# Key sums of an attention kernel: from products with ones on the matrix engine to block transpositions on the vector engine

## What is computed

```
q, k, v = xn @ Wq + bq, xn @ Wk + bk, xn @ Wv + bv     # xn = layernorm(x)
attn = softmax(q @ k.T / 8)                             # over 2048 keys
x = x + layernorm((attn @ v) @ Wo + bo)
```

## Time and profile before

| | us |
|---|---|
| median of 3 runs | 2374.09 (2373.32 to 2374.96) |
| profiled execution | 2373.21 |
| its span | 2371.2 |
| TensorE busy (matmul) | 2339.9 |
| GpSimd busy | 2118.6 |
| VectorE busy | 2064.4 |
| ScalarE busy | 1378.1 |

### The profile page before, as it was taken

The page is one execution under the profiler, slowest core; times in us unless marked ns, Lnnn a source line. Parts: engine busy times, 40 slices in busy tenths (PEclk is TensorE's granted clock), DMA queues, the critical chain, the costliest instruction groups (busy, mean ns, idle before and its releaser), DMA issues.

```text
span 2371.2 us, 43568 instructions
## 1 busy us (share of the span) xinstructions
PE 2339.9 (99%) x15676; PEld 1183.6 (50%) x15676; DVE 2064.4 (87%) x3164; ACT 1378.1 (58%) x1666; POOL 2118.6 (89%) x1220
## 2 busy tenths in 40 slices
PE   8999999999999999999999999999999999999997
PEld 4454554554554545545545545554554544544454
DVE  7888888888888888888888888888888888889987
ACT  6656555555555655655565655656556565555546
POOL 7998989989898989989989898988989988899986
PEclk9999999999999999999999999999999999999999
DMA  2000000000000000100010000100000000110101
GB/s 60 28 17 26 28 24 23 28 21 22 28 29 18 28 24 18 33 28 15 28 31 17 28 28 15 32 28 15 28 28 19 28 28 15 35 33 19 37 28 36
DMA packets 63895, 62.54 MB, mean 26 GB/s; under 512 B 29796, under 2 KB 47588, under 8 KB 63684
## 3 DMA queue, kind: packets, MB, share of 16 engines
q1 hardware_dynamic: 62820, 59.51, 8.3%
q10 hardware_dynamic: 864, 0.26, 0.0%
HBM read 56.88 MB, written 2.61 MB: 25 GB/s over the span
## 4 chain that ended last, share of the span: by engine, by line
PE 92%; POOL 5%; DVE 2%; issue 1%; ACT 0%; DMA 0%; POOLq 0%; DVEq 0%; ACTq 0%
PE o_ps L466 36%; PE spare_ps L421 14%; PE score_ps L445 10%; PE score_ps L451 9%; PE score_ps L448 9%; POOL total L1211 4%; PE spare_ps L407 3%; PE spare_ps L389 3%; PE spare_ps L398 3%; PE spare_ps L511 3%; PE spare_ps L478 1%; DVE max_part L929 1%; DVE ln_stats L901 0%; POOL y_acc L1261 0%; PE score_ps L559 0%
## 5 line engine op out<-in xcount | busy, mean ns | idle before, releaser
L1211 POOL TENSOR_TENSOR total<-total,probs 128x832 f32<-128x832 f32 (+1 forms) x896 | 1761.7, 1966 | 218.4 <-ACT probs L738 142.9
L929 DVE TENSOR_REDUCE max_part<-spare_ps 128x1 f32<-128x512 f32 x2028 | 1303.9, 685 | 261.8 <-PE spare_ps L421 247.9
L738 ACT ACTIVATE probs<-score_ps 128x1024 f32<-128x1024 f32 x1024 | 993.2, 1022 | 812.6 <-PE score_ps L451 812.6
L466 PE MATMUL o_ps<-probs,v_sb 128*64 128x512 f32 x4096 | 979.7, 599 | 0.0
L466 PEld LDWEIGHTS o_ps<-probs,v_sb 128*64 128x64 f32 x4096 | 265.9, 136 | 451.3 <-issue 287.0
L421 PE MATMUL spare_ps<-k_hi,q_hi 64*128 64x512 f32 x2028 | 461.4, 449 | 7.6 <-DVE max_part L929 4.4
L445 PE MATMUL score_ps<-q_hi,kd_hi 64*128 64x512 f32 x2048 | 407.0, 393 | 0.9 <-ACT score_ps L728 0.9
L421 PEld LDWEIGHTS spare_ps<-k_hi,q_hi 64*128 64x128 f32 x2028 | 193.2, 183 | 428.1 <-issue 226.9
L451 PE MATMUL score_ps<-q_hi,kd_lo 64*128 64x512 f32 x2048 | 405.3, 391 | 0.0
L448 PE MATMUL score_ps<-q_lo,kd_hi 64*128 64x512 f32 x2048 | 404.1, 390 | 0.0
L972 DVE TENSOR_REDUCE part_sum<-probs 128x192 f32<-128x768 f32 (+1 forms) x255 | 392.5, 1539 | 1.3 <-ACT probs L738 1.2
(11 more groups left out here) (145 smaller groups left out, 1174.0 us busy)
## 6 DMA issues: line engine op xcount, KB each, us to landing
m_all<-m_scratch SPq DMA_DIRECT2D x64, 512.0 KB, 4.3
denom<-denom_scratch SPq DMA_DIRECT2D x122, 128.0 KB, 2.9
m_scratch<-neg_rows SPq DMA_DIRECT2D x256, 1.0 KB
y_acc<-in_L_attn_x SPq DMA_DIRECT2D x8, 256.0 KB, 6.3
key_f<-in_L_attn_x SPq DMA_DIRECT2D x8, 256.0 KB, 2.7
block_out<-probs SPq DMA_DIRECT2D x8, 256.0 KB, 2.3
denom_col<-denom SPq DMA_DIRECT2D x61, 4.0 KB
denom_scratch<-denom_col SPq DMA_DIRECT2D x61, 4.0 KB, 1.4
```

What stands on the lines that cost most here:

```text
L466: last = nc.tensor.matmul(o_ps[half(h), :], v_sb[:, b, kt, half(h)], probs[:, st % RING, h, :], start=(kt == 0), stop=(kt == T - 1))
L738: nc.scalar.activation(probs[:, st % RING], score_ps[st % 2][:], ACT.Exp, scale=SCALE).then_inc(s["exp_done"], 1)
L929: nc.vector.reduce_max(max_part[:, G % 2, h, qt, kc:kc + 1], bank[max_bank(n, h)], AX.X).then_inc(s["max_done"], 1)
L1211: nc.gpsimd.tensor_tensor(others(total[:, G % 2], G), so_far, others(probs[:, st % RING], G), ALU.add).then_inc(s["sum_done"], 1)
```

## The change

For chunks 0 to 55 (`TURNED` = 64 - 8) the sum over partitions is made without TensorE. VectorE's block transposition turns each 32x32 block of `total` (128x1024) in place of its own (`dve_turn`, into `q_parts`, which is free at that time); a sum along groups of 32 elements gives, for each quarter of the partitions, the sums of 1024 columns (`dve_row_sums`, 128x32); a second transposition (128x32) lays them in rows; four DMAs put the four quarters beside each other on 128 partitions (`sp_quarters`), where VectorE adds them and takes the reciprocal (`dve_quarters`). From there the way is the old one. Chunks 56 to 60 keep the products with ones, and the last three their own way.

Besides, places change: keys d = 4 to 3 (in the first unit 6 and 4 to 3), values 5 to 4, merge 2 to 1, the last part sum of a chunk 1 to 0. For the turned chunks the transposition stands at d = 2, row sums at 4, quarters, reciprocal and the broadcast of the reciprocals at 7, the scaling at d = 4 of the chunk after the next and the output projection at its d = 6. Queries stay at 2. The waits of the old way count from chunk 56 on.

```
-MERGE_AT, L_AT, DENOM_OUT_AT, RECIP_AT, NEG_MAX_AT, NORM_AT = 2, 3, 4, 5, 4, 7
+K_AT = {(0, 3): 0, (1, 0): 1, (1, 3): 2, (2, 3): 3}
+V_AT = {(0, 4): (0, 4), (1, 4): (4, 4), (2, 4): (8, 4), (3, 4): (12, 4)}
+MERGE_AT, L_AT, DENOM_OUT_AT, RECIP_AT, NEG_MAX_AT, NORM_AT = 1, 3, 4, 5, 4, 7
-PART_AT = {3: 0, 5: 1, 6: 2, 1: -1}
+PART_AT = {3: 0, 5: 1, 6: 2, 0: -1}
+TURNED = CHUNKS - 2 * NC
+TURN_AT, ROW_SUM_AT, QUARTERS_OUT_AT, QUARTERS_AT, TURNED_NORM_AT, TURNED_WO_AT = 2, 4, 4, 7, 4, 6
...
+def by_products(G):
+    return TURNED <= G < CHUNKS - COLUMN_CHUNKS
+def by_blocks(G):
+    return 0 <= G < TURNED
...
+        def dve_turn(dve, G):
+            dve.wait_ge(s["sum_done"], (G + 1) * ADDS)
+            dve.wait_ge(s["merge_done"], G + 1)
+            if G:
+                dve.wait_ge(s["rows_summed"], G)
+            else:
+                dve.wait_ge(s["first_split"], FIRST_Q)
+            nc.vector.transpose(q_parts[:].rearrange("p c n -> p (c n)"),
+                                total[:, G % 2].rearrange("p h n -> p (h n)")).then_inc(s["sums_turned"], 1)
+        def dve_row_sums(dve, G):
+            dve.wait_ge(s["sums_turned"], G + 1)
+            if G:
+                dve.wait_ge(s["rows_turned"], G)
+            nc.vector.tensor_reduce(row_sum[:], q_parts[:].rearrange("p c (b i) -> p (c b) i", i=32), AX.X, ALU.add).then_inc(s["rows_summed"], 1)
+            dve.wait_ge(s["rows_summed"], G + 1)
+            if G:
+                dve.wait_ge(s["quarters_in"], 64 * G)
+            nc.vector.transpose(row_turned[:], row_sum[:]).then_inc(s["rows_turned"], 1)
+        def dve_quarters(dve, G):
+            dve.wait_ge(s["quarters_in"], 64 * (G + 1))
+            if G:
+                dve.wait_ge(s["scratch_dma"], 16 * G)
+            nc.vector.tensor_reduce(denom_col[:], denom_quarters[:].rearrange("p a k -> p k a"), AX.X, ALU.add).then_inc(s["quarters_added"], 1)
+            dve.wait_ge(s["quarters_added"], G + 1)
+            nc.vector.reciprocal(denom_col[:], denom_col[:]).then_inc(s["recip_done"], 1)
...
+        def sp_quarters(sp, G):
+            sp.wait_ge(s["rows_turned"], G + 1)
+            if G:
+                sp.wait_ge(s["quarters_added"], G)
+            for a in range(P // 32):
+                sp.dma_start(denom_quarters[:, a, :], row_turned[a * 32:(a + 1) * 32, :]).then_inc(s["quarters_in"], 16)
```

More of the change, by code:

```diff
@@ L63 @@
 WEIGHTS_AT = 2
-FIRST_K_AT = {(0, 6): 0, (1, 0): 1, (1, 4): 2, (2, 4): 3}
-FIRST_V_AT = {(0, 5): (0, 4), (1, 5): (4, 4), (2, 5): (8, 4), (3, 5): (12, 4)}
+FIRST_K_AT = {(0, 3): 0, (1, 0): 1, (1, 3): 2, (2, 3): 3}
+FIRST_V_AT = {(0, 4): (0, 4), (1, 4): (4, 4), (2, 4): (8, 4), (3, 4): (12, 4)}
 FIRST_Q = Q_RING
@@ L108, in projected_at @@
 def projected_at(G, d):
-    if d == WO_AT and 2 <= G < CHUNKS + 2 - COLUMN_CHUNKS:
+    if G < 2:
+        return None
+    if d == (TURNED_WO_AT if G - 2 < TURNED else WO_AT) and G - 2 < CHUNKS - COLUMN_CHUNKS:
         return G - 2
     return None
+def by_products(G):
+    return TURNED <= G < CHUNKS - COLUMN_CHUNKS
+def by_blocks(G):
+    return 0 <= G < TURNED
 def ffn_at(n, stage):
@@ L151, in spare_banks @@
             use("p", g)
-        if d == L_AT and 0 < G <= CHUNKS - COLUMN_CHUNKS:
+        if d == L_AT and by_products(G - 1):
             use("L", G - 1)
@@ L207, in build @@
         denom_4 = sb("denom_4", [P, CH // 2])
+        row_sum = sb("row_sum", [P, 32])
+        row_turned = sb("row_turned", [P, 32])
+        denom_quarters = sb("denom_quarters", [P, P // 32, 2 * TC])
         denom_col = sb("denom_col", [P, CH // HD])
@@ L359, in take @@
                 elif was == "L":
-                    pe.wait_ge(s["denom_copied"], k + 1)
+                    pe.wait_ge(s["denom_copied"], k + 1 - TURNED)
                 elif was == "Wo":
@@ L746, in act_denom @@
         def act_denom(act, G):
-            act.wait_ge(s["denom_ps_ready"], G + 1)
-            if G:
-                act.wait_ge(s["col_dma"], 16 * G)
+            act.wait_ge(s["denom_ps_ready"], G + 1 - TURNED)
+            if G > TURNED:
+                act.wait_ge(s["col_dma"], 16 * (G - TURNED))
             nc.scalar.activation(denom_4[:], bank[SPARE["L", G]][:, 0:CH // 2], ACT.Copy).then_inc(s["denom_copied"], 1)
@@ L974, in dve_part, with total_taken @@
                                     AX.X, ALU.add).then_inc(s["part_done"], 1)
+        def total_taken(eng, G):
+            if by_blocks(G):
+                eng.wait_ge(s["sums_turned"], G + 1)
+            else:
+                eng.wait_ge(s["denom_ps_ready"], G + 1 - TURNED)
+        def dve_turn(dve, G):
[3 more added lines that the diff above has]
+                dve.wait_ge(s["rows_summed"], G)
+            else:
+                dve.wait_ge(s["first_split"], FIRST_Q)
[17 more added lines that the diff above has]
+            nc.vector.reciprocal(denom_col[:], denom_col[:]).then_inc(s["recip_done"], 1)
         def dve_merge(dve, G):
@@ L997, in dve_recip @@
         def dve_recip(dve, G):
-            dve.wait_ge(s["col_dma"], 16 * (G + 1))
+            dve.wait_ge(s["col_dma"], 16 * (G + 1 - TURNED))
             nc.vector.reciprocal(denom_col[:], denom_col[:]).then_inc(s["recip_done"], 1)
@@ L1095, in dve_columns @@
         def dve_columns(dve, G):
-            dve.wait_ge(s["denom_ps_ready"], G + 1)
+            dve.wait_ge(s["denom_ps_ready"], G + 1 - TURNED)
             nc.vector.reciprocal(recip_col[:, G % 2, :], bank[SPARE["L", G]][:, 0:2 * TC]).then_inc(s["denom_copied"], 1)
         def dve_head_y(dve, G):
-            dve.wait_ge(s["denom_copied"], G + 1)
+            dve.wait_ge(s["denom_copied"], G + 1 - TURNED)
             dve.wait_ge(s["wo_ps_ready"], G + 1)
@@ L1134, in dve_program @@
                     dve_centre(dve)
-                if d == RECIP_AT and 0 < G <= CHUNKS - COLUMN_CHUNKS:
+                if d == QUARTERS_AT and by_blocks(G - 1):
+                    dve_quarters(dve, G - 1)
+                if d == RECIP_AT and by_products(G - 1):
                     dve_recip(dve, G - 1)
@@ L1156, in dve_program @@
                     dve_q(dve, G + 2)
+                if d == TURN_AT and by_blocks(G - 1):
+                    dve_turn(dve, G - 1)
+                if d == ROW_SUM_AT and by_blocks(G - 1):
+                    dve_row_sums(dve, G - 1)
                 if n in HEADS_AT:
@@ L1205, in pool_add @@
                 if G >= 2:
-                    pool.wait_ge(s["denom_ps_ready"], G - 1)
+                    total_taken(pool, G - 2)
                 so_far = others(probs[:, (st - 1) % RING], G)
@@ L1336, in pool_program @@
                 G, u, c, d = n // PER_CHUNK, n // (PER_CHUNK * NC), n // PER_CHUNK % NC, n % PER_CHUNK
-                if d == NORM_AT and 0 < G <= CHUNKS - COLUMN_CHUNKS:
+                if d == TURNED_NORM_AT and by_blocks(G - 2):
+                    norm(pool, G - 2)
+                if d == NORM_AT and by_products(G - 1):
                     norm(pool, G - 1)
@@ L1404, in sp_denom_back @@
             sp.wait_ge(s["recip_done"], G + 1)
+            sp.wait_ge(s["denom_dma"], 32 * G)
             sp.dma_start(denom_dram.rearrange("h (p n) -> (h p) n", p=HD), denom_col[:]).then_inc(s["scratch_dma"], 16)
@@ L1452, in sp_program @@
                     sp_ffn_weights(sp)
-                if d == DENOM_OUT_AT and 0 < G <= CHUNKS - COLUMN_CHUNKS:
+                if d == DENOM_OUT_AT and by_products(G - 1):
                     sp_denom_out(sp, G - 1)
@@ L1456, in sp_program @@
                     sp_m_out(sp, G + 1)
-                if d == RECIP_AT and 0 < G <= CHUNKS - COLUMN_CHUNKS:
+                if d == RECIP_AT and by_products(G - 1):
                     sp_denom_back(sp, G - 1)
+                if d == QUARTERS_OUT_AT and by_blocks(G - 1):
+                    sp_quarters(sp, G - 1)
                 if d == M_BACK_AT and G + 1 < CHUNKS:
                     sp_m_back(sp, G + 1)
+                if d == QUARTERS_AT and by_blocks(G - 1):
+                    sp_denom_back(sp, G - 1)
                 for g in ffn_at(n, ST1):
```

9 lines of the change are left out of this document (4 added, 5 removed).

## The result

The changed kernel takes 2393.8 us in the median (five runs, 2391.95 to 2396.98) against 2375.0 for the one before on the same chip: ratio 1.0075, 95% interval 1.0064 to 1.0086. It is slower by 19 us, where 11 us less were forecast.

The account below looks back on a forecast made before the run. TensorE, with 92% of the span, was taken as the bound. Savings of 0.57 and 0.12 us less new stalls gave -0.18 us a chunk, times 56 is -10 us: 2373.2 to 2363 us, range 2350 to 2384.

Parts of the forecast that it names:

- rival 1: Double step 4: row sums run at the part sums' rate, 2.03 us instead of 1.22; 2393 us; chance 0.18, transposition included.
- lateness: Time in us from TensorE's start of a double step's first trial-product pair to VectorE's start on it.
- steps 1, 2 and 6: Double steps of a chunk's attention loop, each opened by a late VectorE; predicted losses 0.09, 0.12 and 0.12 us.
- step 3: Double step after low query and large transposition, which were to make VectorE 0.92 us late; predicted cost 0.12 us.
- the floor: The 0.54 us from TensorE's start of the first pair to VectorE's when VectorE is on time; costs nothing.
- step 7: Double step after output sum and part sum beside the output projection; VectorE at most 0.68 us late, old 0.12 loss gone.
- plain: Said of a double step with no projection; a part sum there was to cost the next double step 0.12 us.
- Rival 2: Stalls in two places, for instance double steps 2 and 4, eat all the gain: 2373 us; 0.14 including a disturbed transfer.
- Rival 3: VectorE's one large item per double step does not stall TensorE: 2335 us; chance 0.12 with what lies toward it.

Follow-up runs that it names:

- the first experiment: The changed kernel with its new places but no block transpositions, all key sums by products with ones on TensorE: 2423.4 us, ratio 1.0194 against the kernel before.

## Why the prediction was wrong

*What held.* TensorE in the loop is the bound. The durations: transposition 1.24 forecast, 1.234 measured; row sums 1.22 and 1.178, so rival 1 did not come. The lateness that each step leaves: 0.89 in steps 1, 2 and 6 (measured 0.88 to 0.90), 0.92 in step 3 (0.95), the floor in 5. (At step 7 it is the floor too, where at most 0.68 was forecast: step 6 lasted longer, so VectorE caught up.) The 0.57 of the products stands in the first experiment's chain. That its chunk of 36.22 is 0.56 longer than the changed one's 35.66 is in part chance, for it loses 0.23 at step 3, and the changed kernel 0.25 at steps 3 and 4. Transfers and GpSimd's additions delayed nothing in the loop.

*The step that failed* is the first one: "So the loss is zero up to about 0.7, 0.12 at 0.89, and above that lateness less 0.80". The 0.12 came from the earlier trace rows, from a step 7 in which no projection stands. I carried it to steps 2, 3 and 6, where one does. There it is 0.17 for queries, 0.20 for keys, 0.17 for values, and 0.29 for outputs, because the projection has a wait of its own, for the bank of A1; the extra 0.1 of the outputs stays open. Steps 2, 3 and 6 have 0.65 together instead of 0.36: 0.29 a chunk. Rows that could have told me stood in my own trace, but I read there a pair without a projection. At step 5 of chunks 58 and 59, beside a value projection, latenesses of 0.99 and 1.22 cost 0.26 and 0.53, where my rule gives 0.19 and 0.42.

*The second step that failed*: "Before, the part sum was plain here, and its 0.12 is gone." It went from step 7 and came back at step 0 as a wait for the seed, 0.10 a chunk. Together 0.39, which is the difference between the forecast chunk (-0.18) and the measured one (+0.19), with 0.02 over.

*The third*: "the new places in the last six chunks, where the key sums stay on TensorE, are put at nothing". What follows chunk 55 took 8 us more, and the old places there gave 7 of them back. The chain over GpSimd in the earlier trace rows said what bound those chunks in the old order; it did not say that nothing else could.

Rival 1's time, 2393, is the measured one by chance: its mechanism, slow row sums, did not come. Rival 2 named waits at steps 2 and 4 that were to eat the gain; the waits were others, and they ate twice as much. Rival 3, no stalls, was the farthest off.

## What to carry to other kernels

A stall's price read at one place holds only for places with the same waits behind it: before moving an item, list for each new neighbour which buffer it must wait for, here which third of the ring. Before counting a stall as gain, look for what is late next within the same length: at step 7 it was ScalarE's seed, only 0.1 behind. With both known, moving the same operations to places with slack turned 0.75% slower into 0.74% faster.

## What was not expected of the hardware

At the start of chunk 61 the changed kernel loses 4.4 us at one stroke. The timeline there shows two VectorE operations with two inputs in SBUF, each of which lasts 0.68 in the kernel before at the same place, and TensorE's next products of two kinds (the first trial products, and the products with the values):

```profile
2222.59 1.86 DVE L1126 TENSOR_TENSOR xn<-y_acc,ln_rstd 128x512 f32<-128x512 f32 x1
...
2225.68 1.69 DVE L1131 TENSOR_TENSOR v_split<-v_f,v_split 32x512 fp32r<-32x512 f32 x1
...
2228.14 0.80 PE L440 MATMUL spare_ps<-k_hi,q_hi 64*128 64x512 f32 x2 [3.06 <-DVE kd_lo L1133]
...
2229.91 3.68 PE L485 MATMUL o_ps<-probs,v_sb 128*64 128x512 f32 x8
```

Both VectorE operations ran beside GpSimd's. So did the same two in the kernel before; what differs is which engine began first. Here the first one began inside a GpSimd addition and ended 0.55 after it (2223.90 and 2224.45), and the second ended 0.56 after the GpSimd addition beside which it began (2226.82 and 2227.38). Before, the first began at 2207.84, just ahead of a GpSimd addition (2207.88): it took 0.68, and the addition 2.48 instead of 1.97. By the Trainium skill (GPSIMD Engine Reference, section Specifications), GpSimd's SBUF interfaces are shared with VectorE, with contention where a VectorE instruction has two SBUF inputs; the durations agree with it, but no run here took GpSimd away. TensorE then stood idle for 3.06 us, and its granted clock fell (stretch in us; its length, then busy time and count of TensorE, weight loads, VectorE, ScalarE and GpSimd; the clock; the DMA share and GB/s):

```profile
2222.00:2228.00 6.00, 3.08 (x20) 1.38 (x16) 5.94 (x6) 2.55 (x4) 6.00 (x4) 0.94 0.02 4
2228.00:2234.00 6.00, 5.86 (x16) 2.25 (x18) 4.04 (x12) 0.95 (x2) 5.69 (x5) 0.50 0.00 0
2234.00:2240.00 6.00, 6.00 (x52) 3.73 (x52) 5.34 (x8) 2.37 (x4) 4.36 (x3) 0.99 0.01 1
```

0.50 is the lower of the two levels, 1.2 GHz: the eight products with the values took 3.68 us instead of 1.94. Before, TensorE is idle for 1.41 at this place. So a wait 1.65 us longer went with a loss of 4.4, and 1.74 of it stands in these eight products at the lower clock. In the four experiments with the new places in the last chunks the two operations lasted 1.82 to 1.90 and 1.68 to 1.69, and the loss was 2.6 to 3.3. With the old places, in four profiles, both lasted 0.68, and the loss was not there. The other surprise is the part sum's rate: four terms cost 1.98 ns an element, 32 terms 1178 / 1024 = 1.15. Why groups of four take longer was not tried.
